# Cross-attention with a gated RMS norm: the gate's memory half in row parts of 512 and 288, each weight tile split once

## What is computed

```python
memory_proj = einsum('bme,de->bmd', memory, W_mem)
scores = einsum('bnd,bmd->bnm', x, memory_proj) / sqrt(D)
attn = softmax(scores)
memory_context = einsum('bnm,bmd->bnd', attn, memory_proj)
gate = sigmoid(einsum('bnf,df->bnd', concat([x, memory_context]), W_gate) + b_gate)
fused = x + gate * memory_context
out = fused * rsqrt(mean(fused**2, -1) + 1e-6) * norm_w
```

## Time and profile before

| what | value |
|---|---|
| median of 3 runs | 306.04 us (305.05 to 307.36) |
| span of the profiled execution | 305.9 us |
| TensorE matmul busy | 293.2 us, 96% of the span |
| VectorE busy | 183.1 us, 60% |
| ScalarE busy | 157.4 us, 51% |
| GpSimd busy | 7.9 us, 3% |

### The profile page before, as it was taken

How to read it: one execution, slowest core, us unless ns; L and a number is a source line. 1 busy time by engine, 2 the same in 40 slices (tenths; PEclk the granted TensorE clock), 3 DMA queues, 4 the chain that set the end, 5 groups by cost and what they waited for, 6 DMA issues and landing times.

```text
span 305.9 us, 4511 instructions
## 1 busy us (share of the span) xinstructions
PE 293.2 (96%) x1658; PEld 281.0 (92%) x1658; DVE 183.1 (60%) x267; ACT 157.4 (51%) x225; POOL 7.9 (3%) x13
## 2 busy tenths in 40 slices
PE   8899999999999999999999999999999999799961
PEld 8899999898989989898998989999999999799961
DVE  3657564557585656758565525334367776748895
ACT  4547345564563936356393506543545566336640
POOL 0000000000000000000000000000000000700010
PEclk9999999999999999999999999999999999979995
DMA  6996291644928386472834011192143334305118
GB/s 204 406 394 221 88 354 47 229 112 121 292 94 291 119 242 213 142 263 97 289 119 159 20 50 69 58 411 98 69 140 137 92 116 137 113 31 181 60 54 268
DMA packets 21198, 50.47 MB, mean 165 GB/s; under 512 B 1712, under 2 KB 5296, under 8 KB 21184
## 3 DMA queue, kind: packets, MB, share of 16 engines
q1 hardware_dynamic: 20096, 49.46, 46.9%
q10 hardware_dynamic: 1088, 0.82, 0.8%
HBM read 47.00 MB, written 3.28 MB: 164 GB/s over the span
## 4 chain that ended last, share of the span: by engine, by line
PE 91%; POOL 2%; DMA 2%; DVE 1%; issue 1%; SPq 1%; ACT 0%; POOLq 0%; DVEq 0%
PE ps L283 67%; PE ps L379 11%; PE ps L355 11%; DMA acc<-xT 2%; PE ps L369 1%; POOL rms_diag L917 1%; POOL rms L912 1%; PE ps L386 1%; PE ps L456 1%; DVE acc L853 1%; DVE act_lo L678 0%; ACT act_hi L493 0%; SPq L223 0%; POOLq L54 0%; PE ps L447 0%
## 5 line engine op out<-in xcount | busy, mean ns | idle before, releaser
L283 PE MATMUL ps<-act_hi,w_hi 128*128 128x400 f32 (+1 forms) x328 | 99.0, 345 | 1.2 <-DVE act_lo L678 1.2
L283 PE MATMUL ps<-act_lo,w_hi 128*128 128x400 f32 (+1 forms) x328 | 98.1, 342 | 0.0
L283 PE MATMUL ps<-act_hi,w_lo 128*128 128x400 f32 (+1 forms) x328 | 98.0, 342 | 0.0
L283 PEld LDWEIGHTS ps<-act_hi,w_hi 128*128 128x128 f32 x328 | 60.9, 190 | 2.7 <-issue 1.5
L283 PEld LDWEIGHTS ps<-act_lo,w_hi 128*128 128x128 f32 x328 | 61.6, 190 | 0.0
L283 PEld LDWEIGHTS ps<-act_hi,w_lo 128*128 128x128 f32 x328 | 61.5, 189 | 0.0
L678 DVE TENSOR_TENSOR w_lo<-w_stage,w_hi 128x1024 fp32r<-128x1024 f32 (+2 forms) x34 | 39.5, 1160 | 26.2 <-ACT w_hi L489 25.5
L489 ACT ACTIVATE w_hi<-w_stage 128x1024 fp32r<-128x1024 f32 x31 | 32.8, 1058 | 37.0 <-PE ps L283 36.6
L678 DVE TENSOR_TENSOR cn_lo<-cn_stage,cn_hi 128x1536 fp32r<-128x1536 f32 (+2 forms) x24 | 28.5, 1217 | 5.2 <-ACT cn_hi L508 5.2
L678 DVE TENSOR_TENSOR ct_lo<-ct_stage,ct_hi 128x1444 fp32r<-128x1444 f32 x16 | 25.8, 1654 | 0.5 <-ACT ct_hi L500 0.5
L581 ACT ACTIVATE pc<-ps,row_inv 100x512 f32<-100x512 f32 x8 | 5.5, 687 | 34.0 <-PE ps L379 34.0
(11 more groups left out here) (71 smaller groups left out, 351.6 us busy)
## 6 DMA issues: line engine op xcount, KB each, us to landing
ct_stage<-ctxT SPq DMA_DIRECT2D x16, 722.0 KB, 9.5
w_stage<-w_gate_mc SPq DMA_DIRECT2D x16, 512.0 KB, 3.5
cn_stage<-ctxN SPq DMA_DIRECT2D x8, 768.0 KB, 5.8
cn_stage<-ctxN SPq DMA_DIRECT2D x8, 512.0 KB
w_stage<-w_gate_x SPq DMA_DIRECT2D x8, 512.0 KB, 8.3
x_again<-xT SPq DMA_DIRECT2D x1, 3200.0 KB, 12.3
acc<-xT SPq DMA_DIRECT2D x7, 400.0 KB, 7.8
w_stage<-w_mem_t SPq DMA_DIRECT2D x4, 512.0 KB, 5.6
```

Source lines behind the costliest of these rows:

```text
L283: done = nc.tensor.matmul(o, wgt, stream[h][part], start=first and wgt is wh and part == 0, stop=last and wgt is wl)
```

## The change

The rows are parted at 512 instead of 400: part 0 is rows 0 to 511 (four chunks of 128 in the norm), part 1 is rows 512 to 799 (three chunks of 96). A step is called by its number n and has a weight tile t and a part g. The order is

```diff
-GROUPS = ((0, NH), (NH, NH // 2), (NH + NH // 2, NH // 2))
+PARTS = ((0, 512), (512, 800))
+CHUNKS = ((4, 128), (3, 96))
+BOTH = 3
+STEPS = [(t, g) for t in range(BOTH) for g in range(2)] + [(t, g) for g in range(2) for t in range(BOTH, KD)]
+W_HOME = (2, 0, 1, 3, 4, 5, 2, 0)
+SPLIT_AT = {0: 2, 2: 3, 4: 4, 6: 5, 7: 6, 8: 7}
...
+            for t in range(1, KD):
+                load_w(J_G2 + t, w_gate_mc[t], t % 2)
...
+            def gate_mc(n, after=None, work=None):
+                t, g = STEPS[n]
+                r0, r1 = PARTS[g]
+                pe.wait_ge(w_lo_done, J_G2 + 1 + t)
+                if n >= 2:
+                    pe.wait_ge(gate_summed, n - 1)
+                o = bank(G2B + n % 2, r1 - r0)
                 for k in range(KD):
...
+                    done = three([o], w_tile(W_HOME[t], k), [(act_hi[:, k, r0:r1], act_lo[:, k, r0:r1])],
+                                 k == 0, k == KD - 1)
+                    if k == after:
+                        work()
                 done.then_inc(gate_made, 1)
...
+            def mean_0():
+                pe.wait_ge(summed, END0 + 1)
...
+            def mean_1_most():
+                pe.wait_ge(summed, LAST)
...
+            def mean_1_rest():
+                pe.wait_ge(last_squared, 1)
...
             def inverse(g):
+                n, rows = CHUNKS[g]
+                pe.wait_ge(diag_done, CHUNKS[0][0] + g * CHUNKS[1][0])
...
-            gate_mc(KD + 1, 1, 1, between=(2, lambda: mean_square(0, KD)))
-            gate_mc(KD + 2, 1, 0, between=(2, lambda: inverse(0)))
...
+            for n in range(END0 + 2):
+                gate_mc(n)
+            gate_mc(END0 + 2, 4, mean_0)
+            gate_mc(END0 + 3)
+            gate_mc(END0 + 4, 1, lambda: inverse(0))
+            gate_mc(END0 + 5)
+            mean_1_most()
+            mean_1_rest()
+            inverse(1)
```

ScalarE's order for each step n is: the high part of tile `SPLIT_AT[n]` if there is one, the sigmoid of n, then square and norm weight of n - 1 (at n = 11 and 15 these two come before the sigmoid). VectorE's order:

```diff
+            for n in range(END0 + 1):
+                gate_sum(n)
+                if n in SPLIT_AT:
+                    split_gate_w(SPLIT_AT[n])
+                gate_times(n)
+                if n > 0:
+                    sum_squares(n - 1)
+                fuse(n)
+            sum_squares(END0)
...
+            gate_sum(END0 + 2)
+            mean_plus_eps(0)
+            gate_times(END0 + 2)
+            sum_squares(END0 + 1)
+            fuse(END0 + 2)
+            gate_sum(END0 + 3)
+            gate_times(END0 + 3)
+            sum_squares(END0 + 2)
+            fuse(END0 + 3)
+            dve.wait_ge(rooted, 1)
+            diagonals(0)
+            gate_sum(END0 + 4)
+            gate_times(END0 + 4)
+            sum_squares(END0 + 3)
+            fuse(END0 + 4)
+            dve.wait_ge(weighted, END0 + 1)
+            dve.wait_ge(inv_made, 1)
+            for k in range(3):
+                output(k, 1, 0)
+            sum_squares(END0 + 4)
+            gate_sum(LAST)
+            output(3, 1, 0)
+            gate_times(LAST)
+            fuse(LAST)
+            dve.wait_ge(fused, LAST + 1)
+            part = acc[:, STEPS[LAST][0], slice(*PARTS[1])]
+            nc.vector.tensor_tensor(square[:, LAST % 2, 0:part.shape[1]], part, part,
+                                    ALU.mult).then_inc(last_squared, 1)
+            output(4, 1, 0)
+            mean_plus_eps(1)
+            output(5, 1, 0)
+            dve.wait_ge(rooted, 2)
+            diagonals(1)
+            output(6, 2, 0)
+            dve.wait_ge(weighted, LAST + 1)
+            dve.wait_ge(inv_made, 2)
             for k in range(0, KD, 2):
-                output(k, 2, 2)
+                output(k, 2, 1)
```

More of the change, by code:

```diff
@@ L421, in _ @@
             mc_block(3, 1, True)
-            def gate_mc(t, h, slot, first=False, part=slice(0, H), psum=None, between=None):
-                if part.start == 0:
-                    pe.wait_ge(w_lo_done, J_G2 + 1 + t)
-                if not first:
-                    pe.wait_ge(gate_summed, t - 1 + (part.start > 0))
+            def gate_mc(n, after=None, work=None):
[5 more added lines that the diff above has]
+                o = bank(G2B + n % 2, r1 - r0)
@@ L430, in gate_mc @@
                 for k in range(KD):
[L431 removed]
+                    if n == 0:
                         pe.wait_ge(mc_lo_done, k + 1)
[L433 to L436 removed]
@@ L633, in finish @@
-            def finish(t, k, h, slot, part=slice(0, H), between=None):
-                act.wait_ge(fused, t + 1)
-                if not isinstance(t, int) or t >= 2:
-                    act.wait_ge(summed, t - 1)
-                rows = acc[:, bass.ds(k, 1), h * H + part.start:h * H + part.stop].rearrange("p k r -> p (k r)")
-                nc.scalar.activation(square[:, slot, part], rows, ACT.Square).then_inc(squared, 1)
-                if between is not None:
-                    between()
-                act.wait_ge(squared, t + 1)
-                nc.scalar.activation(rows, rows, ACT.Copy, scale=norm_t[:, bass.ds(k, 1)]).then_inc(weighted, 1)
@@ new lines, in sum_squares, with gate_sum @@
+            def sum_squares(n):
+                rows = square_sum[:, slice(*PARTS[STEPS[n][1]])]
+                dve.wait_ge(squared, n + 1)
+                if n > 0:
+                    dve.wait_ge(summed, n)
+                nc.vector.tensor_tensor(rows, rows, square[:, n % 2, 0:rows.shape[1]], ALU.add).then_inc(summed, 1)
+            def gate_sum(n):
+                t, g = STEPS[n]
+                rows = acc[:, t, slice(*PARTS[g])]
+                dve.wait_ge(gate_made, n + 1)
+                nc.vector.tensor_tensor(gate[:, n % 2, 0:rows.shape[1]], bank(G2B + n % 2, rows.shape[1]), rows,
+                                        ALU.add).then_inc(gate_summed, 1)
@@ new lines, in gate_times, with fuse @@
+            def gate_times(n):
+                t, g = STEPS[n]
+                rows = mc[:, t, slice(*PARTS[g])]
+                part = gate[:, n % 2, 0:rows.shape[1]]
+                dve.wait_ge(gate_done, n + 1)
+                nc.vector.tensor_tensor(part, part, rows, ALU.mult).then_inc(gated, 1)
+            def fuse(n):
+                t, g = STEPS[n]
+                rows, xa_rows = (a[:, t, slice(*PARTS[g])] for a in (acc, x_again))
+                dve.wait_ge(gated, n + 1)
+                nc.vector.tensor_tensor(rows, gate[:, n % 2, 0:rows.shape[1]], xa_rows, ALU.add).then_inc(fused, 1)
```

289 lines of the change are left out of this document (111 added, 178 removed).

## The result

The changed kernel took 310.64 us (310.61 to 310.72) against 306.51 for the kernel before: ratio 1.0135, 95% interval 1.0098 to 1.0172. A second set of executions gave 309.87 against 306.43, ratio 1.0123 (1.0085 to 1.016). It is slower by over 1%, and by more than the forecast's range allowed. The profiled execution has a span of 308.8 us, where 308.0 was forecast, so 0.8 of the miss lies in the span. The larger part lies around it: this execution took 310.67 us, 1.87 more than its span.

The account below looks back on a forecast made before the run. TensorE, busy 96%, was taken as the bound. Steps 0 to 13 end at 282.54; diagonals 3.35, inverse 1.30, matmuls 2.45 and clock 1.3 give 290.9; a tail of 17.1 gives 308.0 us, range 305.2 to 309.8.

Parts of the forecast that it names:

- the line of the tail: After step 14 VectorE's chain of sums, norm and outputs, then stores, sets the end: 17.1 us from T14.
- a long step, a short step: Gate steps of 24 matmuls: 5.52 us at 512 columns (0.230 each), 3.26 us at 288 (0.136 each).
- wait before the first inverse: Six matmuls into step 14, TensorE stands 2.53 us for VectorE's diagonals, made after the fuse of step 13.
- first inverse: In step 14, TensorE's `inverse(0)` of 4 x 128 columns takes 1.30 us, from 1.14 for 4 x 100.
- low clock in steps 14 and 15: After the wait the clock falls as before: 1.65 us lost, 1.3 in step 14, the rest in step 15.
- the last mean: In the tail, TensorE's last mean matmuls take 0.79 us.
- The power, taken as 2.42: First norm's power on GpSimd takes 2.42 us and is ready before the diagonals need it, near T11 + 10.3.
- That span is 0.14 below the median, which I leave out: The profiled span of 305.9 us was taken as 0.14 below the median time, and the difference ignored.
- the first (the clock holds through the gate): Rival: the wait comes but the clock holds through the gate; T14 289.6, end 306.8; chance 0.17.
- The second (a longer low clock): Rival: low clock lasts to the last gate matmul, 42 matmuls at 0.24; end 310.0; chance 0.13.
- The third (the change does what it says): Rival: diagonals ready in time, no wait and no clock drop; T14 287.1, end 304.3; chance 0.06.
- Worth nothing: Half the weight loads and splits gone, eight times 1.22 us on VectorE, all beside TensorE: no gain.

Follow-up runs that it names:

- after_again: The changed kernel with no edit, run in more executions; 309.87 us.
- last_sum_earlier: The changed kernel with one of the three long outputs ahead of the last step's sum moved behind it; 309.09 us.
- diag_before_sum: The changed kernel with the first norm's four diagonals moved ahead of the sum of step 13; 305.87 us.
- after_wait_filled: The changed kernel with 38 small bfloat16 matmuls into an unused bank just ahead of the first inverse; 308.30 us.
- four_splits_more: diag_before_sum with four weight tiles split once more on ScalarE and VectorE in steps 9 to 12, result unused; 306.43 us.
- outputs_earlier: diag_before_sum with the three long outputs moved ahead of the sum of step 14; 304.89 us.
- outputs_earlier_warm_tail: outputs_earlier with 30 and 26 small bfloat16 matmuls in TensorE's two idle times of the tail; 304.34 us.
- parts_of_400: diag_before_sum with the rows parted at 400 instead of 512, four chunks of 100 in each norm; 307.68 us.

## Why the prediction was wrong, though its mechanism came true

The wait, the fall of the clock and the line of the tail were the ones forecast. From the timeline of the changed kernel, with T14 the end of step 14's slots:

| term | forecast | measured |
|---|---|---|
| a long step, a short step | 5.52, 3.26 | 5.59, 3.20 |
| steps 0 to 13 with the mean | 64.36 | 64.73 (218.31 to 283.04) |
| wait before the first inverse | 2.53 | 2.49 |
| first inverse | 1.30 | 1.13 |
| low clock in steps 14 and 15 | 1.65 | 1.40, all in step 14 |
| T14 | 290.9 | 291.26 |
| last sum after T14 | 4.57 | 4.54 |
| first of the last outputs after T14 | 11.3 | 11.78 |
| from there to the span's end | 5.8 | 5.76 |
| span | 308.0 | 308.8 |

The length of a long step is read from the sums of steps 7, 8 and 9, each released by TensorE; they are 5.58 and 5.62 apart:

```profile
255.98 0.69 DVE L826 TENSOR_TENSOR gate<-ps,acc 128x512 f32<-128x512 f32 x1 [2.18 <-PE ps L282]
...
261.56 0.69 DVE L826 TENSOR_TENSOR gate<-ps,acc 128x512 f32<-128x512 f32 x1 [1.95 <-PE ps L282]
...
267.18 0.69 DVE L826 TENSOR_TENSOR gate<-ps,acc 128x512 f32<-128x512 f32 x1 [1.99 <-PE ps L282]
```

That is 0.233 per matmul, outside the bounds of 0.228 to 0.231; the 288 columns came at 0.133, below the lower bound of 135 ns, and the two errors nearly cancel, which is luck. The Trainium skill's rule for loading a stationary tile (TensorE: Matmul & The Clock Gate, LDWEIGHTS), by which the load would not hold the short matmuls up, is compatible with the 0.133. The trace does not confirm its figure: the loads of the 128x128 tiles start 0.133 us apart in the short steps, but each is recorded with 0.19. In the tail the mis-sized term is the last mean, 1.12 us for 0.79: the clock was already low there (1.74 us of idleness ahead of it), and I had taken the low clock for the inverse alone.

```profile
298.35 1.12 PE L462 MATMUL ps<-mean_w,square 128*96 128x1 f32 x6 [1.74 <-DVE square L901]
...
301.31 1.60 PE L471 MATMUL ps<-rms_diag,ones 96*128 96x96 f32 x6 [1.84 <-DVE rms_diag L852]
```

That too differs between executions: behind the same wait the mean takes 1.12 us in the traces of after_again, last_sum_earlier and diag_before_sum, and 0.67 in those of after_wait_filled and four_splits_more (1.74 or 1.75 us of wait in all six traces, the changed kernel's included).

The first inverse came near its 1.30 by luck as well. The forecast scaled the 1.14 of the earlier trace rows, which holds the drain; the next matmul of the kernel before started 0.91 behind the inverse:

```profile
267.14 0.43 PE L283 MATMUL ps<-act_hi,w_hi 128*128 128x400 f32 x1
```

At full clock the first inverse takes 0.92 behind the wait and 0.81 without one (after_again, diag_before_sum). The 1.13 of the table holds some 0.2 of the low clock. The power, taken as 2.42, took 1.03, which changed nothing, since nothing waited for it.

The step that failed is the sentence "That span is 0.14 below the median, which I leave out". I took the difference between one execution's span and the median of three others for what lies around a span. It is 1.75 to 1.88 us in every execution of every kernel here. With it the same sum gives 308.0 + 1.8 = 309.8, against 309.87 and 310.64 measured. The 0.8 left against the first set, whose four executions all have the lower mean clock as the forecast assumed, is the 0.36 of T14 and the 0.44 behind it, in the table above. That the second set is met to 0.1 is luck, since two of its executions pull the median down. The 0.14 was small only because the profiled execution came from the slower half of the kernel before's executions, 1.7 us above the other half. That has a second consequence which the forecast missed. "I take the same 1.65 us lost" compared the changed kernel with that one execution. By their mean clocks the kernel before loses the clock in only about half its executions, the changed kernel in eight of ten. So even with the forecast's own sum the change is not 2.1 us but 309.8 against a median of 306.4, 3.4 us or 1.1%, where I gave 0.77 to no change. Measured were 4.1 and 3.4 us.

The rivals: the first (the clock holds through the gate) is true of two executions in ten, if their mean clock is read rightly. The second (a longer low clock) did not occur; eleven matmuls, as before ten. The third (the change does what it says) is what diag_before_sum shows for the kernel that was meant, and its time of 305.87 is 1.6 above the rival's 304.3, which lacks the same 1.8 around the span. "Worth nothing" for the halved splits holds to 0.56 us for four of them. That the tail was VectorE's line was right for the changed kernel and for outputs_earlier. But the stores were close behind: where the line alone was shortened further, in last_sum_earlier and outputs_earlier_warm_tail, the stores of part 0 held the end, and the forecast had the stores as the last link only.

Not tried: a last part smaller than 288 rows, since the first part already fills a bank of 512 columns of this kernel.

## What to carry to other kernels

Before a span is turned into a time, find what lies around it from executions that have both, and ask which of its executions a profile shows: a kernel whose granted clock dips in some executions has times in groups, and one profile is a draw from them. When two medians differ by about as much as their traces say, compare the traces stretch by stretch all the same; here sums agreed that had different parts. Where an instruction of TensorE waits for a small product of VectorE, place it by counting back from when that product can be ready; two lines moved were worth 4 us here, the restructuring around them nothing. When a bound in a tail is removed, read the DMA share behind it before the next edit: an output moved forward gains nothing while a large store stands in front of it.

## What the runs showed of the hardware

A wait of 1.80 us in TensorE, with the norm's small matmuls behind it, brought its clock from 2.4 to 1.2 GHz in both traces of the kernel before, and by mean clock and time in about half of its executions; a wait of 2.49 us in both traces of the changed kernel, and by the same reading in eight of ten. A wait of the same length filled with small bfloat16 matmuls did not in its trace (1.00 in step 14). In the tail one and the same wait of 1.74 or 1.75 us ahead of the last mean went with a mean of 1.12 us, at the low clock, in four traces and with one of 0.67 in two.

The first power on GpSimd, 4 columns, took 2.42 us in the kernel before. It took 1.03 in the changed one, with 128 partitions and, in parts_of_400, with 100, so the size is not the reason. It took 2.11 in four_splits_more, where a split of 1.23 us on VectorE starts with it, as one does beside the power of the kernel before. So a VectorE subtraction of 1024 columns, running at the same time, about doubles the time of this small GpSimd instruction. Why is not shown by these runs.
